# Cross attention in a fused decoder: maxima from scores by queries, exponentials from scores by keys, operands stacked on partitions

## The reference

```python
def _L1_xattn_ref(q, k, v, gamma):        # q = layernorm(x), k = v = ctx; each (8, 256, 512)
    h = N_HEAD                            # 8 heads
    qh = q.reshape(B, h, 32, 512)         # the 256 TOKENS are split over heads, 32 each
    kh = k.reshape(B, h, 32, 512)
    vh = v.reshape(B, h, 32, 512)
    scale = 1.0 / sqrt(32)
    qk = einsum('bhdq,bhdl->bhql', qh, kh) * scale    # 512 x 512 scores, contraction over 32
    sm = softmax(qk, axis=-1)
    ret = einsum('bhql,bhdl->bhdq', sm, vh)           # (32, 512) per head
    return gamma * ret.reshape(B, 256, 512)
```

## Time and profile before

| what | value |
|---|---|
| median of three runs | 3319.01 us |
| the profiled execution's own time | 3320.24 us |
| its span | 3318.5 us |
| PE busy | 3040.6 us (92%) |
| DVE busy | 2341.7 us (71%) |
| ACT busy | 1598.7 us (48%) |
| POOL busy | 806.5 us (24%) |
| cross attention of the mixers, four stretches | 111.0, 101.3, 100.5, 88.1 us |

### The profile page before, as it was taken

How to read it: one execution, slowest core, us unless ns; L and a number is a source line. 1 busy time by engine, 2 the same in 40 slices (tenths; PEclk the granted TensorE clock), 3 DMA queues, 4 the chain that set the end, 5 groups by cost and what they waited for, 6 DMA issues and landing times. The chain is left out here.

```text
span 3318.5 us, 61052 instructions
## 1 busy us (share of the span) xinstructions
PE 3040.6 (92%) x22689; PEld 2441.5 (74%) x22689; DVE 2341.7 (71%) x4405; ACT 1598.7 (48%) x3656; POOL 806.5 (24%) x968
## 2 busy tenths in 40 slices
PE   7999999997998799999999869899999979999999
PEld 5666566664887688888888746666667668888888
DVE  5666666665665588888888666877786867777776
ACT  3333333333221455555555336556565746555555
POOL 1221122112554111111111142341423012222222
PEclk9999999998998899999999979999999989999999
DMA  6324233221111677777777621211110032222222
GB/s 260 127 80 170 102 128 127 99 94 39 46 40 33 205 243 242 242 240 244 249 247 243 235 67 58 81 56 58 45 59 20 8 122 92 74 74 77 74 74 71
DMA packets 144825, 401.85 MB, mean 121 GB/s; under 512 B 39056, under 2 KB 47760, under 8 KB 131680
## 3 DMA queue, kind: packets, MB, share of 16 engines
q1 hardware_dynamic: 106176, 323.30, 28.4%
q0 software_dynamic: 18976, 50.45, 5.1%
q10 hardware_dynamic: 19456, 25.18, 2.2%
HBM read 344.09 MB, written 54.76 MB: 120 GB/s over the span
## 5 line engine op out<-in xcount | busy, mean ns | idle before, releaser
L1465 POOL DMA_INDIRECT xg<-normed_rows,idx x128 | 126.8, 991 | 669.4 <-PE psum L1547 578.9
L2651 POOL TENSOR_TENSOR mixf<-act 128x256 f32<-128x256 f32 x128 | 143.7, 1123 | 474.6 <-DVE act L2927 474.6
L174 POOL TENSOR_SCALAR ve<-mv 128x1 f32<-128x1 f32 x112 | 37.2, 332 | 833.0 <-DVE mv L774 585.4
L1562 PE MATMUL psum<-xT_hi,wgu_hi 128*128 128x192 f32 (+1 forms) x1536 | 228.6, 271 | 4.2 <-ACT aT_lo L1529 4.2
L1562 PE MATMUL psum<-xT_lo,wgu_hi 128*128 128x192 f32 (+1 forms) x1536 | 223.3, 268 | 0.0
L1562 PE MATMUL psum<-xT_hi,wgu_lo 128*128 128x192 f32 (+1 forms) x1536 | 222.9, 267 | 0.0
L1601 DVE TENSOR_TENSOR wgu_lo<-wgu,wgu_hi 128x1408 fp32r<-128x1408 f32 x128 | 202.7, 1625 | 22.8 <-ACT wgu_hi L1489 22.7
L1562 PEld LDWEIGHTS psum<-xT_hi,wgu_hi 128*128 128x128 f32 (+1 forms) x1536 | 190.8, 183 | 28.8 <-ACT wgu_hi L1489 21.5
L1502 ACT ACTIVATE eth<-psum 128x192 f32<-128x192 f32 (+1 forms) x192 | 63.4, 330 | 298.3 <-PE psum L1562 298.3
L2019 ACT ACTIVATE scratch<-psum,smin 128x512 f32<-128x512 f32 x256 | 173.8, 686 | 60.1 <-DVE smin L2411 56.9
L2411 DVE TENSOR_REDUCE smin<-psum 128x2 f32<-128x1024 f32 x128 | 155.5, 1217 | 61.8 <-PE psum L2173 38.5
(11 more groups left out here) (436 smaller groups left out, 8601.0 us busy)
## 6 DMA issues: line engine op xcount, KB each, us to landing
wgu<-in_w_gu_dram SPq DMA_DIRECT2D x64, 1408.0 KB, 6.1
w_slot<-w_split SPq DMA_DIRECT2D x21, 2048.0 KB
wd<-in_w_d_dram SPq DMA_DIRECT2D x64, 512.0 KB, 8.6
w_raw<-in_w_dram SPq DMA_DIRECT2D x128, 256.0 KB, 2.6
expert_out<-yo ACTq DMA_DIRECT2D x64, 256.0 KB, 5.2
w_slot<-w_split SPq DMA_DIRECT2D x28, 512.0 KB
wd<-in_w_d_dram SPq DMA_DIRECT2D x64, 192.0 KB, 9.0
w_split<-w_slot SPq DMA_DIRECT2D x4, 2048.0 KB
```

Source lines behind the costliest of these rows:

```text
L1465: pool.indirect_dma_start(out=xg[b][0:w, t, :], out_offset=None, in_=rows, in_offset=bass.IndirectOffsetOnAxis(ap=idx[b][0:w, t:t + 1], ax ...
L1562: ins = pe.matmul(bank(2 + m)[0:w, gu * CAP:(gu + 1) * CAP], wgu2[b][wp][:, gu, kc, m0:m0 + w], xT2[b][xp][:, kc, :], start=(i == 0 and kc ...
L2651: pool.tensor_tensor(mixf[:, g % LAG, :], act2[:, g % LAG, 0, :], act2[:, g % LAG, 1, :], ALU.add).then_inc(sy["f_mix"], 1)
```

## The change

Only `mixers` is changed. Three things are new.

First, the three products become one. The parts are stacked on partitions: `keys` holds per head 32 rows of the context's high part, the same again, and 32 rows of its low part; `queries` holds high, low, high. One product over 96 partitions (`KROWS`) gives the sum of the three. [...]

Second, the scores are computed twice. `maxima_scores` computes them by queries, for the maximum alone; DVE reduces them to `tops` (32 items of two products a pair). When the eight items of four heads are through, `turn_maxima` turns the 16 columns of maxima, DVE splits them into high and low parts (`shift`), and `place_shift` puts these by DMA into two further rows of `queries`; the same rows of `keys` hold minus one. `turned_scores` then computes the scores by keys over 98 rows, so that the maximum is already subtracted, and ACT takes the exponential with no bias straight into `probT`. The transposes of probabilities, their copies by ACT and DVE and the accumulated sums are gone.

Third, the sums come from a product: `returned` multiplies the probabilities by 32 columns of ones into bank 7 and by the context into bank 6, four heads side by side, 512 columns long, 16 steps a pair. `returned_copy` on ACT takes both out; `turn_sums`, `recips`, `turn_recips` and `attended` follow.

The maxima and the turns run in an order given by two tables: `LEAD`, the first 12 items, before any step, and `PLAN`, which places the other items in three slots of each of 16 steps. A unit u is a half sequence; u 0 and 1 are the first sequence's.

```diff
+KROWS = 3 * LD
+QUADS = 16
+LEAD = tuple(("max", 0, m) for m in range(8)) + (("turn", 0, 0),) + tuple(("max", 1, m) for m in range(3))
+PLAN = {0: ([("max", 1, 3)], [("max", 1, 4)], []), 1: ([("max", 1, 5)], [("max", 1, 6)], []),
+        2: ([("max", 1, 7)], [], [("turn", 1, 0)]), 3: ([("max", 2, 0)], [("max", 2, 1)], []),
...
 @ SP
+            def stack_keys(s):
...
+                for j in range(NT):
+                    for r in range(HPT):
+                        rows, hd = slice(r * LD, (r + 1) * LD), j * HPT + r
+                        for at, part in ((0, cx_hi[rows, j, :].bitcast(F32)), (LD, cx_hi[rows, j, :].bitcast(F32)),
+                                         (2 * LD, cx[rows, j, :])):
+                            sp.dma_start(keys[b][at:at + LD, hd, :].bitcast(F32), part).then_inc(sy["keys_in"], 16)
...
+            def place_shift(p, u):
+                s, g, b = group(p, u)
+                sp.wait_ge(sy["item_used"], ITEMS * p + ORDER.index(("turn", u, 0)) + 1)
+                for part in range(2):
+                    sp.dma_start(queries[b][KROWS + part:KROWS + part + 1, g * HPT:(g + 1) * HPT, :].bitcast(F32),
+                                 shift[u % 2][:, part, :].bitcast(F32)).then_inc(sy["shift_in"], 16)
...
+                stack_keys(first)
                 load_cx(second)
+                for j in range(NT):
+                    stack_queries(first, j)
+                place_shift(p, 0)
+                for j in range(NT):
+                    stack_queries(second, j)
+                stack_keys(second)
                 if p + 1 < npair:
-                    sp.wait_ge(sy["cx_lo_ready"], second + 1)
                     load_cx(second + 1)
...
+                for u in range(1, 4):
+                    place_shift(p, u)
 @ ACT
             def decays(k):
+                if k % (2 * MH) == 0:
+                    act.wait_ge(sy["keys_in"], KEYS_IN * (k // MH + 1))
...
+            def exponentials(n, r):
+                e = 4 * n + r
+                act.wait_ge(sy["turned_psum"], e + 1)
+                if n >= 2 and r == 0:
+                    act.wait_ge(sy["ret_psum"], n - 1)
+                act.activation(probT(n // QUADS, e % 8), bank(4 + e % 2), ACT.Exp).then_inc(sy["sexp_ready"], 1)
 @ PE
+            def maxima_scores(p, u, m, at):
+                s, g, b = group(p, u)
+                if m == 0:
+                    pe.wait_ge(sy[f"queries_in{g}"], QUERIES_IN * (s + 1))
+                    pe.wait_ge(sy["keys_in"], KEYS_IN * (s + 1))
+                hd = g * HPT + m // 2
+                for k in range(2):
+                    lc = 2 * (m % 2) + k
+                    ins = pe.matmul(bank_pair(2 * (at % 2))[:, k, :], queries[b][0:KROWS, hd, lc * P:(lc + 1) * P],
+                                    keys[b][0:KROWS, hd, :], start=True, stop=True)
+                ins.then_inc(sy["item_psum"], 1)
...
+            def turned_scores(p, n, r):
+                s, g, b = group(p, n // 4)
+                hd, mc, e = g * HPT + r, n % 4, 4 * (QUADS * p + n) + r
+                if mc == 0 and r == 0:
+                    pe.wait_ge(sy["shift_in"], 32 * (4 * p + n // 4 + 1))
+                if e >= 2:
+                    pe.wait_ge(sy["sexp_ready"], e - 1)
+                pe.matmul(bank(4 + e % 2), keys[b][0:KROWS + 2, hd, mc * P:(mc + 1) * P],
+                          queries[b][0:KROWS + 2, hd, :], start=True, stop=True).then_inc(sy["turned_psum"], 1)
...
+                for n in range(QUADS + 1):
+                    for part in range(3):
+                        if n < QUADS and part < 2:
+                            turned_scores(p, n, 2 * part)
+                            turned_scores(p, n, 2 * part + 1)
+                        if n and part == 2:
+                            returned(p, n - 1)
+                        for _ in PLAN[n][part] if n < QUADS else ():
+                            at += 1
+                            item(p, at)
```

More of the change, by code:

```diff
@@ L1711, in mixers @@
         cx, cxT = sb("cx", [P, NT, D]), two("cxT", [P, KC, S])
-        h2 = [[sb(f"h_{part}{b}", [P, NT, D], F32R) for part in ("hi", "lo")] for b in range(2)]
-        cx2 = [[sb(f"cx_{part}{b}", [P, NT, D], F32R) for part in ("hi", "lo")] for b in range(2)]
+        h_hi = [t[:].rearrange("p c t -> p (c t)").rearrange("p (j d) -> p j d", j=NT).bitcast(F32R) for t in hT]
+        keys = two("keys", [P, LH, D], F32R)
+        tops, shift = two("tops", [P, 2, QUADS]), two("shift", [QUADS, 2, P], F32R)
+        rec = sb("rec16", [P, QUADS])
         yk = sb("yk", [P, NT * TOPK, D])
@@ L1883, in _ @@
             norm(1, norm1(1))
+            pool.wait_ge(sy["rstd_ready"], NT * (norm1(1) + 1))
+            for b in range(2):
+                sy.link(pool, "pool_link", pool.memset(keys[b][minus, :, :].bitcast(F32), -1.0))
             for p in range(npair):
@@ new lines, in _ @@
+                residual(first, 0)
+                second_stats(first, 0)
+                second_apply(first, 0)
+                residual(first, 1)
+                second_stats(first, 1)
+                low(first, 0)
+                second_apply(first, 1)
+                low(first, 1)
+                for at in range(len(LEAD)):
+                    item(p, at)
+                    if at in (1, 5):
+                        residual(second, at // 4)
+                    if at in (2, 6):
+                        second_stats(second, at // 4)
+                    if at in (4, 7):
+                        second_apply(second, at // 4 - (at == 4))
+                    if at in (6, 9):
+                        low(second, at // 9)
```

418 lines of the change are left out of this document (220 added, 198 removed).

## The result

The changed kernel takes 3416.39 us (median of four runs, 3414.16 to 3421.65), the kernel before on the same chip 3318.18. The ratio is 1.0295, with a 95% interval of 1.028 to 1.031: 98 us slower. The prediction said 3348 us, slower by 29, with a range up to 3374. The direction was right, the size was not. The profiled execution has a span of 3413.1 us, 94.6 more than before. The mixers account for it: their first maximum comes 9.5 us later than the first score did, and from there to the last addition they take 727.9 us for 641.1, together 96.

The account below looks back on a forecast made before the run. TensorE was taken as nearly full, the other engines close behind. Pair by pair, -3.8, +5.9, +6.7 and +20.4 gave +29 us on a median of 3319.01: 3348 us, range 3306 to 3374.

Parts of the forecast that it names:

- step 4: Start of this step of a pair's sixteen, after slow work behind the key wait: put at 51 us from the pair's start.
- step 3, SP's order: SP's queue: 48 query and key DMAs behind the first shift, 0.48 us each, 23.0 us; keys land at 46.4.
- The wait itself: TensorE, at the second sequence's first maximum, waits 11.5 us a pair for that sequence's keys to land.
- steps 0 to 2: First three of a pair's sixteen steps, behind the first turned product: 10.6 us together, ending at 34.4.
- Step 1, the stacking: Start of a pair: queries stacked by 12 DMAs per half sequence on SP's queue; first maximum starts at 5.3 us.
- Step 2, the lead: Exponentials need all maxima of four heads: first turned product at 23.8 us, ScalarE doing nothing for 21.5 us.
- Step 4, the steps: Sixteen steps a pair, set by TensorE-ScalarE handoffs over two banks: 4.2 us each, 3.8 without a maximum.
- a full TensorE between 51 and 104: Sign that the prediction is wrong: TensorE being the full engine from 51 to 104 us of a pair.
- The second rival: Handoffs shorter than read, so steps run at TensorE's load, 3.6/2.7 us: -39 us in all, 3310; chance 0.14.
- The first rival: Stacking DMAs follow by their bytes, 0.18 us each, and the key wait vanishes: -65 us, 3284; chance 0.13.
- The third: Rival: TensorE's clock stays low in the steps, 7 us each: 3495, or 3385 if one in four; chance 0.10.
- The fourth: Rival: the change does not do what it says, e.g. first pair's decays wait for keys: +10 us, 3358.

Follow-up runs that it names:

- e1: Changed kernel with the second sequence's 24 key DMAs cut into 48 of 16 rows each, same bytes: 1.0569 times the kernel before, +69 us against the changed kernel.
- e2: Changed kernel issuing only 8 of the second sequence's 24 key DMAs in pairs 2 to 4: 1.0277 times the kernel before, -26 us against the changed kernel.
- e8: Changed kernel with second sequence's keys issued right behind the first shift, ScalarE issuing its first half of queries, first maxima awaiting two heads' queries: 1.0145 times the kernel before.
- e9: e8 with second sequence's keys split before its normalisation and issued by ScalarE, SP issuing all queries, GpSimd's fills of minus one later: 1.0033 times the kernel before.
- e15: The kernel of e9 run again, on a chip of the same sort: 1.0023 times the kernel before, -86 us against the changed kernel.
- e4: Changed kernel with the product with ones only in every fourth step: 1.0296 times the kernel before, -20 us against the changed kernel.
- e11: e9 with the product with ones only in every fourth step: 0.9931 times the kernel before.
- e7: Changed kernel with 40 extra score products on TensorE ahead of its wait for second sequence's keys: 1.0388 times the kernel before, +10 us against the changed kernel.
- e10: e9 with the first group's eight maxima taken over 128 of 512 keys: 1.0017 times the kernel before.
- e16: e9 with VectorE's second residual, statistics, normalisation behind the shift, key issues shared 18 ScalarE, 6 SP, ScalarE's last rounding after four exponentials: 1.0033 times the kernel before.
- e3: Changed kernel with the second sequence's 24 query DMAs issued by ScalarE instead of SP: 1.0251 times the kernel before, -35 us against the changed kernel.

## Why the prediction was right in direction and wrong in size

Piece by piece on the prediction's scale, means over the four pairs; each is the time from the piece before:

| piece | forecast | measured | times four |
|---|---|---|---|
| first maximum, after the first score of before | 5.3 | 5.7 | +1.5 |
| first turned product | 18.5 | 21.9 | +13.8 |
| second sequence's first maximum | 22.6 | 31.4 | +35.3 |
| step 4 | 4.6 | 5.8 | +4.8 |
| next time steps (last pair: last addition) | 56.5 | 59.4 | +11.6 |

Together 67 us, and with the 29 forecast 96; the span says 94.6.

**The mis-sized term is step 3, SP's order, by its price of an issue.** The mechanism, that 48 DMAs stand between the first shift and the keys' landing, was right, and so was the wait. From the first of the 50 DMAs (the shift's two among them) to the last issue are 49 intervals: 23.5 us at 0.48, and 31.0 at the measured 0.633. The four pairs took 32.2, 32.4, 33.4 and 31.0, so the price alone is 7.5 us a pair, 30 of the 35 in the table's third row; the rest is in issues of the first three pairs that took longer (in the first, eight DMAs 6.67 us for 4.96). I took the pitch of loads from DRAM for copies within SBUF, and bounded it by the same rows, 0.43 to 0.52. The bound was too narrow: no row of before showed such a copy. Even those rows I read low: their starts are 0.52 and 0.51 us apart, and 0.48 is the length of one. e1 and e2 show the price from both sides. e8 and e9, 69 and 86 of the 98 us back, show what order and queues were worth together with the earlier start, whose share, by the waits for queries, is some 15 us. The landing took 3.35, 2.0, 2.0 and 2.2 us, on the mean the 2.4 that was taken.

The wait itself came out near the forecast, 13 against 11.5 us, only because what stood ahead of it was late as well. From the first turned product to TensorE's stop it took 20.3, 20.5, 20.4 and 12.6 us, where steps 0 to 2 were forecast at 10.6. In the first three pairs the "remote" stop lies in it, and ScalarE's exponentials with it:

```profile
2061.06 0.59 ACT L2097 ACTIVATE xn<-psum 128x512 f32<-128x512 f32 x1
2068.61 1.09 ACT L2097 ACTIVATE scratch<-psum 128x512 f32<-128x512 f32 x2 [6.96 <-remote]
```

The prediction saw such stops in the earlier trace rows and gave its own stretches none, and it gave steps 0 to 2 the full clock, where 0.67 to 0.75 was granted in these pairs. In this kernel both misses are hidden under the wait for keys. They are a part of why the loss did not turn into a gain when that wait went: with early keys a pair takes 99 to 104 us from its first maximum (e15), where the prediction's own terms without the wait give 89 (107.2 less 5.3, 11.5 and 1.5).

**Step 1, the stacking**, was near: from the first issue to the first maximum 8.9 us (2024.03 to 2032.93), forecast 8.3. The offsets of the four pairs are 9.5, 2.5, 3.3 and 7.4 us, and the first holds 1.8 us by which the mixers as a whole start later and 2.2 of GpSimd's fills (the second time steps start 37.7 us after the first, before 35.4), inside the bounds of 0 to 3 us that were given for the fills. The fourth pair's 7.4, 2.1 over the forecast, was not explained.

**Step 2, the lead**, was 3.4 us short: 1.7 for the normalisation that GpSimd blocks, which no step had. The rest I put down to TensorE at a clock of 0.66 between the reductions, which no run separated. ScalarE's long idleness came as said: its exponentials start 22 us after the first maximum.

**Step 4, the steps**, had the right length for the right reason, though the busy share says otherwise. From 2092.41 to 2148, at full clock, they take 4.4 us with maxima (4.2 forecast) and 4.0 without (3.8). TensorE is 97% busy there, where the prediction had it 85% busy at work, and it had named a full TensorE between 51 and 104 as a sign against it. By the share the sign came, but the rows show waits in it. A step at full clock:

```profile
2096.83 0.73 PE L2300 MATMUL psum<-queries,keys 98*128 98x512 f32 x2
2097.40 0.63 PE L2254 MATMUL psum<-keys,queries 96*128 96x512 f32 x2
2098.02 0.98 PE L2300 MATMUL psum<-queries,keys 98*128 98x512 f32 x2
2098.84 0.63 PE L2254 MATMUL psum<-keys,queries 96*128 96x512 f32 x2
2099.39 1.07 PE L2314 MATMUL psum<-scratch,ones 128*32 128x512 f32 x8
2100.28 1.04 PE L2320 MATMUL psum<-scratch,cxT 128*32 128x512 f32 x8
```

Eight fp32 products take 1.86 us (0.89 and 0.97), as the earlier trace rows gave them, 1.78. A score product takes the 0.23 to 0.24 us of the earlier trace rows where nothing is awaited: the groups of two are 0.63 long, and one record is 0.39. But the second group of turned products is 0.98 long, and the rows of ScalarE and of the weight loads (PEld) in the same step say why:

```profile
2097.37 1.08 ACT L2097 ACTIVATE scratch<-psum 128x512 f32<-128x512 f32 x2 [2.15 <-PE psum L2300]
2098.01 0.19 PEld L2300 LDWEIGHTS psum<-queries,keys 98*128 98x128 f32 x1 [0.42 <-ACT scratch L2097]
2098.50 0.19 PEld L2300 LDWEIGHTS psum<-queries,keys 98*128 98x128 f32 x1 [0.30 <-ACT scratch L2097]
```

The third turned product waits for the first exponential and the fourth for the second, 1.18 and 1.67 us into the step; the prediction had 1.15 and 1.63. In a step without maxima the wait stands in TensorE's own rows, and the third product comes at the same point, 1.19 us, with nothing between:

```profile
2129.71 0.74 PE L2300 MATMUL psum<-queries,keys 98*128 98x512 f32 x2
2130.90 0.99 PE L2300 MATMUL psum<-queries,keys 98*128 98x512 f32 x2 [0.45 <-ACT scratch L2097]
```

So the first pair of maxima is done within a wait, and the handoffs set the first half of a step. By these prices TensorE's own load is about 3.8 us of 4.4 with maxima and 2.8 of 4.0 without (an estimate: eight or four products of 0.24 and 1.86). The busy share is higher because the end of a record is modelled and reaches over the short waits. e4 and e11 do not speak against it, as said there. One term of the step doesn't follow from its row and came out right even so: four products of four columns are 1.2 us by the earlier trace rows, 0.9 was taken, and 0.91 was measured (2101.25 to 2102.16).

**The second rival** (steps at TensorE's load) did not come: its steps of 3.6 and 2.7 us would lack the waits that the rows show. **The first rival** (issues hidden by their bytes) is refuted by the 0.633 us of the changed kernel's own rows and by e1. What the Trainium skill says of it, in DMA: Bandwidth & Descriptors, section Issuing engines are not separate DMA queues, that the sequencer's time is usually small relative to the transfer, doesn't hold for such copies: 0.633 us of issue against 0.18 of bytes (an estimate, 64 KB at the 362 GB/s of the earlier trace rows), and a second issuing engine was worth 35 us. **The third** (low clock) came around the stops only: in the first pair the clock is 0.59 to 0.68 in the lead, steps 0 to 3 and the first products behind the wait, where a pair of products takes 0.85 us and not 0.55 at the clock's lower level (0.50 from 2055.6 to 2060.7), and 1.00 in all that follows. Behind the wait it cost 1.9 us a pair (5.8 us for what takes 3.85 in the step above, 2097.40 to 2101.25; 1.5 forecast). Its share in the lead and in steps 0 to 2 was not told apart, since e7 failed to keep the clock up. **The fourth** (decays wait for keys) didn't come: ScalarE has no wait for keys in the trace.

## What to carry to other kernels

Rearranging data over partitions by many small DMAs costs the issuing queue a fixed time each, 0.633 us here, so count the DMAs behind which an awaited one stands, and price them by a row of their own kind; a load from DRAM is no such row. If they can't be fewer, issue them before the wait they are queued behind, and over the queue of an engine that idles at that moment. Whether an engine could have moved the rows in place of the DMAs was not tried. A busy share near 100% does not prove that an engine is the limit: look for a wait in its weight loads, and whether the same instruction comes at the same point of a step with less work ahead of it. A test that takes work out of a queue's own order doesn't tell a full engine from a waiting one. And a change that takes work from all engines but makes one of them wait for all maxima first must be charged for the idle lead, 22 us a pair here; that it ate up what the steps saved is the reading that fits, and e10 and e16, which shortened the lead, got nothing for it beyond the uncertainty.

## What the runs showed of the hardware

- A copy of 32 rows by 2 KB within SBUF is issued in 0.59 us and every 0.633 us, by SP and (0.64) by ScalarE; one of 16 rows the same. The last of a row of them landed 2.0 to 3.35 us after its issue began. Two engines issuing together slow each other little: 0.63 and 0.64 us in e9; in e3 SP's mean was 0.71 to 0.75 in the three pairs in which GpSimd gathered as well and 0.64 in the fourth.
- VectorE's 128x512 normalisation took 2.27 us and not 0.54 beside a GpSimd subtraction of 2.35 us, and when e9 moved the subtraction, the normalisation that it then ran beside took 2.56 and the other 0.54; beside GpSimd's gathers, in e9, it took 0.54.
- Score products of 96 to 98 rows by 512 columns, both operands new each time, follow every 0.23 to 0.24 us at full clock where they wait for nothing, and every 0.43 us at a granted clock of 0.50 (2055.6 to 2060.7 of the changed kernel). Four fp32 products of 32 output rows by 512 columns side by side take 0.89 to 0.97 us at full clock (two records each).
- On chips of sort A the kernel before and the changed kernel stop for 6.7 to 8.1 us in each of the first three pairs, released by an event of no instruction; no trace of sort B has such a stop.
- The same two kernels took 3255 and 3374 us on one chip, 3318 and 3416 on another. The ratio moved from 1.029 to 1.036, which is more than its interval, so ratios of different chips are to be compared with care.
